# Order of gather and scatter in GpSimd's queue, in the last stage of a four-layer graph network

## The chip, the core and the metric

The kernel runs on one core of a Trainium2 chip. The metric is the device time of one execution in microseconds (us), from the first to the last instruction with what lies around them. The core's engines are named as in the profile: PE (TensorE, matmuls; PEld is its weight load), DVE (VectorE), ACT (ScalarE), POOL (GpSimd, here almost only the issuer of indirect DMAs) and SP (SyncE, the issuer of plain DMAs). Each engine works through its own list of instructions and waits on semaphores for the others.

## The reference

A graph of 100,000 nodes with 64 features each and 50,000 edges (src, dst), sorted by dst, goes through four residual layers. LN is a layer norm over the 64 features, and `sum` adds up the edges of one destination node:

```
h = relu(LN(x));  x = x + S(S(h))             S(h)[d] = sum(edge_weight * h[src])
h = relu(LN(x));  x = x + norm * sum(norm * (h @ W)[src]) + self loop + bias
h = relu(LN(x));  x = x + relu((h + sum(h[src])) @ W1.T + b1) @ W2.T + b2
h = relu(LN(x));  m = relu([h[src], h[dst], edge_attr] @ mW1 + mb1) @ mW2 + mb2
                  x = x + relu([h, sum(m)] @ uW1 + ub1) @ uW2 + ub2
```

All matrices are small (64 to 160 rows, 64 or 128 columns) and all data float32.

## The kernel before, in words

The edges lie in 128 partitions by 392 columns (391 and one more), in order of their destination. A *unit* is 14 columns (`G`), that is 128 x 14 edges; there are 28 units, and a *step* is two of them, b = 0 and b = 1, so 14 steps (`STEPS`), numbered 0 to 13. Every tile that is written as `name[b]` exists once for each b and serves all the steps: `ga[b]`, `acc[b]`, `isl[b]` and `osl[b]` among them.

The stages follow each other: preparation and ranks, two hops of layer 1 with scattered sums, a dense pass that computes all layers for all nodes as if they had no edges and writes `out`, two passes that sum the messages of layers 2 and 3 into `tables[0]` and `tables[1]`, and the **last stage**, which the change touches. It takes the edges from the last column to the first, computes for each edge layers 2 and 3 of its source and its destination, layer 4 with the message network (`m0`, `m1`: two halves of seven columns) and the update network (`u0`, `u1`), and scatters the new rows of those nodes that have edges to `out`.

The last stage is software-pipelined on PE, ACT and DVE. Each of the three runs `last_pass(None)` once and then `last_pass(i)` for i = 0 to 13; this text calls them *pass* i. In pass i an engine finishes step i (messages, running sums, update network) and in between prepares step j = i + 1. What matters here, in the order of the lists:

- DVE, pass i: line 2031 adds `us[b] = hin[b] + ga[b]` for step i + 1, where `ga` holds the gathered sums of `tables[1]`. When both additions are done it raises `ga_free` of step i + 1 (each b by itself). Later come the running sums of step i + 1 over `x3[b]` (line 1658, tile `zx`), which overwrite `x3` and so wait for `acc_ready` of step i; between that of b = 0 and that of b = 1 the update's first half is added to `acc` (line 1998, `u0`). The second half (`u1`) is added last in the pass, and then `o_ready` of step i is raised: `acc[b]` holds the finished rows.
- ACT, pass i: after its work for step i + 1 it copies `acc[b] = x3[b]` for b = 0 and b = 1 (line 1441) and raises `acc_ready`. Before each copy it waits until the scatter of step i - 1 has landed, since that reads `acc[b]`. Behind the two copies in its list stand the PSUM copies and rectifiers of the update network:

```
if not first:
    act.wait_ge(tt.written[b], 16 * G * i)
tt.acc_ready.raise_by(nc.scalar.copy(flat(acc[b]), flat(x3[b])), ("a", b))
...
copy(tt, i, "u0")
relu(tt, i, "u0", 2)
```

- PE, pass i: transposes and matmuls in the order m0, m1, the products of step i + 1, u0, u1.
- SP loads the tiles of step i + 2 in pass i and stores the running message sums.
- POOL: `t_gather(j)` waits for `ga_free` of step j - 1 for b = 0, copies 14 indices to `isl[0]` (line 768), issues 14 indirect DMAs of 128 rows into `ga[0]` (line 772), and does the same for b = 1. `t_scatter(i)` waits for `o_ready` of step i, copies indices to `osl[b]` and issues 14 indirect DMAs from `acc[b]` to `out` (line 908), for b = 0 and then b = 1. Before, the list was: gather 0, 1, 2, scatter 0, gather 3, then for i = 2 to 11 in a loop scatter i - 1 and gather i + 2, then scatters 11, 12, 13.

Of the kernel before, what the change touches and what calls it, by code (L numbers as in the profile page):

```python
# [126 lines left out]
def gnn(nc, x, src, dst, edge_attr, edge_weight, W1g, b1g, W2a, b2a, W2b, b2b, mW1, mb1, mW2, mb2, uW1, ub1,  # L127
        uW2, ub2, out):
    ctx = ExitStack()
    with ctx:  # L130
# [344 lines left out]
        def tcol(i, b):  # L475
            return (U - 1 - b) * G - 2 * G * i
# [230 lines left out]
        def _(pool):  # L707
# [58 lines left out]
            def slot_copy(o, i_):  # L766

                return nc.gpsimd.tensor_copy(o, i_).then_inc(s_slot, 1)  # L768

            def gather(o, table, idx, limit, s, columns=range(G)):  # L770
                for g in columns:
                    nc.gpsimd.indirect_dma_start(  # L772
                        o[:, g, :], None, table, bass.IndirectOffsetOnAxis(idx[:, g:g + 1], 0),
                        bounds_check=limit, oob_is_err=False).then_inc(s, 16)
# [116 lines left out]
            def t_gather(i, slots, first=False):  # L891
                for b in B2K:
                    if not first:
                        after.wait_ge(*tt.ga_free.at(i - 1, ("g", b)))
                    slot_copy(isl[b][:, :], ptr_i[:, bass.ds(tcol(i, b), G)])
                    after.wait_ge(s_slot, base + slots + b + 1)
                    gather(ga[b], tables[1], isl[b], rows_max, tt.got_a[b])

            def t_scatter(i, slots, first=False):
                for b in B2K:  # L900
                    after.wait_ge(*tt.o_ready.at(i, ("o", b)))
                    if not first:

                        after.wait_ge(tt.written[b], 16 * G * i)
                    slot_copy(osl[b][:, :], out_idx[:, bass.ds(tcol(i, b), G)])
                    after.wait_ge(s_slot, base + slots + b + 1)
                    for g in range(G):
                        nc.gpsimd.indirect_dma_start(  # L908
                            out, bass.IndirectOffsetOnAxis(osl[b][:, g:g + 1], 0), acc[b][:, g, :], None,
                            bounds_check=nodes_max, oob_is_err=False).then_inc(tt.written[b], 16)  # L910
# [3 lines left out]
            t_gather(0, 0, True)  # L914
            t_gather(1, 2)
            t_gather(2, 4)
            t_scatter(0, 6, True)
            t_gather(3, 8)
            with pool.Fori(2, STEPS - 2) as i:
                t_scatter(i - 1, 4 * i + 2)  # L920
                t_gather(i + 2, 4 * i + 4)
            for i in (STEPS - 3, STEPS - 2, STEPS - 1):
                t_scatter(i, 2 * STEPS + 2 * i)

# [1216 lines left out]
```

## Time and profile before

| what | value |
|---|---|
| time, median of 3 runs | 6286.37 us (6284.91 to 6287.19) |
| the profiled execution: its time | 6285.3 us |
| its span, first to last instruction | 6283.5 us |
| POOL busy, share of the span | 3393.1 us, 54% |
| PE busy | 3762.4 us, 60% |
| DVE busy | 3494.4 us, 56% |
| ACT busy | 1775.1 us, 28% |
| the last stage: from its first gather, 4870 us, to the end | about 1,413 us |
| the same stretch, busy: PE, DVE, POOL, ACT | 1008, 965, 876, 531 us |

Shares of busy time average over stages with different limits. The rows further down are of the last stage and show one pass in the middle of it, the first passes and the last. In a row of the timeline the first number is the start in us from the start of the span, the second the duration, then the engine, the line, the operation, the tiles (output before the arrow) and how many instructions are merged; in brackets stands how long the engine was idle before, and what ended that.

### The profile page before, as it was taken

Reading aid. Unit: us, or ns where it says so; the run is one execution under the profiler, and the core shown is the slowest. Engines: PE = TensorE matmul, PEld = TensorE weight load, DVE = VectorE, ACT = ScalarE, POOL = GpSimd, SP = SyncE. Lnnn points to the kernel's source line nnn. Section 1 sums busy time; section 2 is a strip of 40 time slices with the busy share of each in tenths; the row PEclk is TensorE's granted clock in tenths of the full one; section 3 lists DMA queues with packets and bytes.
Section 4 is the critical chain, followed back from the end, with each engine's and each line's share of the span. In section 5 each row is a group of like instructions: output and inputs, shape, how many; then the busy total and the mean of one; then the engine's idle time right before and its main releaser. Section 6 shows DMA issues by size and latency. Waiting matters only on the chain.

```text
span 6283.5 us, 70156 instructions
## 1 busy us (share of the span) xinstructions
PE 3762.4 (60%) x19038; PEld 3090.1 (49%) x19150; DVE 3494.4 (56%) x7361; ACT 1775.1 (28%) x3984; POOL 3393.1 (54%) x2949
## 2 busy tenths in 40 slices
PE   4756665654888888788888830001211577777775
PEld 2444444434888888666666630001111466666664
DVE  5434434433444444578888854443555677777773
ACT  2433443430000000344444420000100334434432
POOL 3777777764555555400000037767775566766763
PEclk9766666665555555699999975555555788888887
DMA  3232223232222222211111112222333322222220
GB/s 121 48 57 48 48 48 57 48 66 25 24 23 23 23 24 21 42 47 47 47 47 47 47 62 94 94 102 99 133 124 124 108 71 88 92 64 88 94 62 16
DMA packets 318644, 398.99 MB, mean 63 GB/s; under 512 B 206217, under 2 KB 223719, under 8 KB 317990
## 3 DMA queue, kind: packets, MB, share of 16 engines
q1 hardware_dynamic: 142518, 309.97, 14.0%
q0 software_dynamic: 176000, 87.72, 10.8%
q14 instruction: 93, 0.76, 0.0%
q8 instruction: 33, 0.54, 0.0%
HBM read 219.85 MB, written 212.39 MB: 69 GB/s over the span
## 4 chain that ended last, share of the span: by engine, by line
PE 24%; issue 21%; POOL 20%; DVE 16%; DMA 10%; ACT 4%; DVEq 1%; POOLq 0%; SPq 0%; ACTq 0%
POOL ga L772 14%; DMA hop<-acc,osl 8%; PE tp L1095 6%; PE tp L1082 5%; POOL hop L810 4%; PE tp L967 4%; PE mm L1015 3%; DVE xc L1620 2%; PE mm L948 2%; DVE cc L1658 2%; DVE wide L1799 1%; PE tp L941 1%; DVE st L1617 1%; DVE h L1640 1%; DVE wide L1794 1%
## 5 line engine op out<-in xcount | busy, mean ns | idle before, releaser
L772 POOL DMA_INDIRECT ga<-table,isl x784 | 836.3, 1067 | 271.5 <-issue 231.0
L846 POOL DMA_INDIRECT xu<-acc,osl x392 | 613.7, 1566 | 488.8 <-issue 452.7
L810 POOL DMA_INDIRECT hop<-acc,osl x392 | 632.8, 1614 | 194.4 <-issue 130.8
L1256 ACT ACTIVATE sq<-xc 128x896 f32<-128x896 f32 x280 | 266.2, 951 | 1289.6 <-DVE xc L1620 1283.6
L768 POOL COPY isl<-map_idx 128x14 int32 (+1 forms) x28 | 6.4, 228 | 1082.0 <-DMA ms<-h 1080.7
L1082 PE MATMUL tp<-us,wide 128*128 128x64 f32 x1568 | 416.9, 422 | 268.3 <-DVE wide L1799 268.3
L1029 PE MATMUL tp<-us,wide 128*128 128x64 f32 x1568 | 341.1, 422 | 369.2 <-DVE us L1640 369.2
L1029 PEld LDWEIGHTS tp<-us,wide 128*128 128x128 f32 x1568 | 336.6, 333 | 376.5 <-issue 376.5
L1082 PEld LDWEIGHTS tp<-us,wide 128*128 128x128 f32 x1568 | 380.0, 332 | 276.5 <-DVE wide L1799 166.5
L1617 DVE TENSOR_REDUCE st<-ga 128x14 f32<-128x896 f32 x56 | 60.8, 1085 | 781.9 <-DMA ga<-in_x,isl 610.1
L908 POOL DMA_INDIRECT out_x<-acc,osl x392 | 422.8, 1079 | 133.9 <-issue 113.0
L772 POOL DMA_INDIRECT ga<-in_x,isl x392 | 414.9, 1058 | 119.8 <-issue 81.4
L772 POOL DMA_INDIRECT ga<-xu,isl x392 | 401.6, 1025 | 138.9 <-issue 117.8
L1794 DVE TENSOR_SCALAR wide<-mm,key_slot 128x256 f32<-128x256 f32 x392 | 188.0, 480 | 510.8 <-PE mm L1019 475.1
L1044 PE MATMUL tp<-xw,cc 128*128 128x394 f32 x784 | 396.6, 599 | 93.7 <-ACT found L1350 93.4
L1095 PE MATMUL tp<-acc,wide 128*128 128x64 f32 x1560 | 423.4, 427 | 0.8
L1375 ACT ACTIVATE acc<-tp,h 128x64 f32<-128x64 f32 x392 | 101.5, 310 | 1072.7 <-PE tp L1095 958.9
L1267 ACT COPY vt<-tp 128x896 f32<-128x896 f32 x224 | 199.4, 906 | 684.2 <-PE tp L941 682.5
L1095 PEld LDWEIGHTS tp<-acc,wide 128*128 128x128 f32 x1560 | 372.4, 329 | 20.2 <-ACT acc L1375 5.5
L941 PE MATMUL tp<-ident,us 128*128 128x128 f32 x392 | 84.9, 404 | 486.7 <-DVE us L1929 486.5
L1000 PE MATMUL tp<-acc,mh 128*128 128x64 f32 x4 | 1.3, 435 | 577.4 <-DMA hsum<-table,head_i 577.4
L1626 DVE TENSOR_REDUCE st<-sq 128x14 f32<-128x896 f32 x280 | 294.5, 1085 | 76.2 <-ACT sq L1256 74.6
(327 smaller groups left out, 9332.6 us busy)
## 6 DMA issues: line engine op xcount, KB each, us to landing
wide<-xu SPq DMA_DIRECT2D x56, 448.0 KB, 3.3
table<-acc SPq DMA_DIRECT2D x56, 448.0 KB, 2.5
xin<-xs SPq DMA_DIRECT2D x56, 448.0 KB, 4.5
wide<-table SPq DMA_DIRECT2D x56, 448.0 KB
xu<-in_x SPq DMA_DIRECT2D x25, 1000.0 KB, 5.7
hop<-zeros SPq DMA_DIRECT2D x1, 12544.0 KB, 35.6
xu<-ga SPq DMA_DIRECT2D x28, 448.0 KB, 2.6
hin<-hop SPq DMA_DIRECT2D x28, 448.0 KB, 3.3
```

The costliest lines, as they stand in the source:

```text
L772: nc.gpsimd.indirect_dma_start(o[:, g, :], None, table, bass.IndirectOffsetOnAxis(idx[:, g:g + 1], 0), bounds_check=limit, oob_is_err=Fals ...
L810: nc.gpsimd.indirect_dma_start(hop, bass.IndirectOffsetOnAxis(osl[b][:, g:g + 1], 0), acc[b][:, g, :], None, bounds_check=hop_max, oob_is_ ...
L846: nc.gpsimd.indirect_dma_start(xu, bass.IndirectOffsetOnAxis(osl[b][:, g:g + 1], 0), acc[b][:, g, :], None, bounds_check=all_max, oob_is_e ...
L908: nc.gpsimd.indirect_dma_start(out, bass.IndirectOffsetOnAxis(osl[b][:, g:g + 1], 0), acc[b][:, g, :], None, bounds_check=nodes_max, oob_i ...
L967: t = nc.tensor.matmul(o[:, at - c + j * w:at - c + j * w + w], src_[:, j * P:j * P + P], weights, start=False, stop=j == (c + n) // w - 1)
L1029: t = nc.tensor.matmul(o[:, g * D:g * D + D], equal[b][:, c, (g % 2) * P:(g % 2) * P + P], us[b][:, c, :], start=n == 0, stop=n == 1)
L1044: f.key_row.raise_by(nc.tensor.matmul(tp[1][:, at:at + KEYS], reach[:, g * P:g * P + P], key_steps, start=True, stop=True), ("g", b, g))
L1082: t = nc.tensor.matmul(o, equal_run[:, 2 * q + n, mine:mine + P], us[b][:, 2 * q + n, :], start=n == 0, stop=alone and n == 1)
L1095: t = nc.tensor.matmul(o, equal_run[:, c, 2 * P + mine:3 * P + mine], passed[:, c, :], start=False, stop=n == 1)
L1256: f.squared.raise_by(nc.scalar.activation(full(lane_s[q]), full(lane_c[q]), ACT.Square), (n, q))
L1626: f.variance.raise_by(V.tensor_reduce(st[q][:, 1, :], full(lane_s[q]), X, ALU.add), (n, q))
L1794: V.tensor_scalar(equal_run[:, g, 0:2 * P], mm[half][:, here * P:here * P + 2 * P], key_slot[b][:, g:g + 1], None, ALU.is_equal)
```

## The change

In POOL's list the gather of the sums two steps ahead is put ahead of the scatter of the results one step behind, in the loop and in the two items ahead of it. The second argument is the number of index copies made so far, on which each waits, and follows the order. Nothing else changes, and the other engines' lists are the same.

```
@@ -914,11 +914,11 @@
             t_gather(0, 0, True)
             t_gather(1, 2)
             t_gather(2, 4)
-            t_scatter(0, 6, True)
-            t_gather(3, 8)
+            t_gather(3, 6)
+            t_scatter(0, 8, True)
             with pool.Fori(2, STEPS - 2) as i:
-                t_scatter(i - 1, 4 * i + 2)
-                t_gather(i + 2, 4 * i + 4)
+                t_gather(i + 2, 4 * i + 2)
+                t_scatter(i - 1, 4 * i + 4)
             for i in (STEPS - 3, STEPS - 2, STEPS - 1):
                 t_scatter(i, 2 * STEPS + 2 * i)
```

## Rows read from the trace of the kernel before

**Rows 1.** The page, GpSimd's busy tenths in 40 slices; the last stage is the last nine.
```profile
POOL 3777777764555555400000037767775566766763
```

**Rows 2.** Waits from 5000 us on: who waited for whom, total us, times, longest.
```profile
POOL osl L768 <- DVEq L75: 206.9, 14, 53.0
...
ACT acc L1441 <- DMA out_x<-acc,osl: 11.9, 1, 11.9
```

**Rows 3.** Line 2031 on VectorE over the whole run.
```profile
L2031 DVE TENSOR_TENSOR us<-hin,ga x28: 1082/1086/1093, 4909.4 to 6115.8; 128x896 f32<-128x896 f32 x28
its engine sat idle before it (us, times) until:
```

**Rows 4.** VectorE in order of time, one pass: start, us, engine, line, operation, idle before.
```profile
5459.80 2.09 DVE L2031 TENSOR_TENSOR us<-hin,ga 128x896 f32<-128x896 f32 x2
...
5498.28 1.14 DVE L1658 SCALAR_TENSOR_TENSOR zx<-zx,more,wide 128x64 f32<-128x64 f32 x3
...
5553.35 2.10 DVE L2031 TENSOR_TENSOR us<-hin,ga 128x896 f32<-128x896 f32 x2
```

**Rows 5.** GpSimd in order of time, the same pass.
```profile
5423.97 0.19 POOL L768 COPY osl<-out_idx 128x14 int32 x1 [10.47 <-DVEq L75]
...
5465.31 0.23 POOL L768 COPY isl<-ptr_i 128x14 int32 x1
5466.40 1.99 POOL L772 DMA_INDIRECT ga<-table,isl  x1 [0.86 <-POOL isl L768]
...
5517.48 0.19 POOL L768 COPY osl<-out_idx 128x14 int32 x1 [10.47 <-DVEq L75]
```

**Rows 6.** ScalarE in order of time, the same pass.
```profile
5485.21 1.77 ACT L1441 COPY acc<-zx 128x896 f32<-128x896 f32 x2
5489.67 1.90 ACT L1267 COPY vt<-tp 128x896 f32<-128x896 f32 x2 [2.69 <-PE tp L941]
```

**Rows 7.** Pass 13, the chain that ended last.
```profile
6207.43 2.15 DMA out_x<-acc,osl
```

**Rows 8.** GpSimd, its two DMA lines: ns, minimum, median and maximum of one.
```profile
L772 POOL DMA_INDIRECT ga<-table,isl x784: 991/997/1985, 4240.7 to 6066.2; - x196
...
L908 POOL DMA_INDIRECT out_x<-acc,osl x392: 982/983/1911, 5050.5 to 6264.5; - x196
```

**Rows 9.** Gather of step 2 in pass 0: VectorE's line 2031, then GpSimd.
```profile
4994.91 2.09 DVE L2031 TENSOR_TENSOR us<-hin,ga 128x896 f32<-128x896 f32 x2
...
4996.13 0.93 POOL L768 COPY isl<-ptr_i 128x14 int32<-128x14 int32 x1 [45.30 <-DVEq L75]
...
4999.95 1.00 POOL L772 DMA_INDIRECT ga<-table,isl  x1 [0.30 <-issue]
```

**Rows 10.** Pass 13, GpSimd and ScalarE in order of time.
```profile
6171.99 0.20 POOL L768 COPY osl<-out_idx 128x14 int32<-128x14 int32 x1 [52.97 <-DVEq L75]
6172.46 0.98 POOL L908 DMA_INDIRECT out_x<-acc,osl  x1 [0.28 <-POOL osl L768]
...
6196.74 0.94 ACT L1441 COPY acc<-zx 128x896 f32<-128x896 f32 x1
6209.60 0.94 ACT L1441 COPY acc<-zx 128x896 f32<-128x896 f32 x1 [11.92 <-DMA out_x<-acc,osl]
```

**Rows 11.** TensorE, then VectorE: first row of the pass above, the others of pass 13.
```profile
5490.63 3.27 PE L948 MATMUL mm<-vt,u 128*128 128x512 f32 x8
...
6211.39 5.74 PE L948 MATMUL mm<-vt,u 128*128 128x512 f32 x8 [5.12 <-ACT vt L1267]
...
6220.56 0.62 DVE L1998 TENSOR_TENSOR acc<-acc,tp 128x448 f32<-128x448 f32 x1 [1.07 <-PE tp L967]
```

**Rows 12.** Pass 13 by windows: busy us (instructions) by engine, PEclk, DMA share, GB/s.
```profile
6211.00:6216.00 5.00, 4.61 (x6) 2.19 (x7) 0.00 (x0) 2.15 (x3) 0.00 (x0) 0.50 0.00 0
...
6217.30:6230.00 12.70, 11.62 (x82) 9.46 (x80) 2.49 (x4) 4.70 (x5) 0.63 (x2) 1.00 0.00 1
```

**Rows 13.** The chain of waits from 5400 to 5600, shares by line.
```profile
by line: issue 26.5%; PE tp L967 14.8%; PE mm L948 8.8%; DVE cc L1658 8.3%; DVE zx L1658 5.9%; PE mm L952 4.7%; DVE xc L1620 4.5%; PE tp L941 4.2%; ACT zx L1272 4.1%; DVEq L1658 2.9%; PE tp L965 2.1%; DVE us L2051 2.0%; DVE h L2046 1.3%; DV
```

## The prediction

> **What bounds the kernel now.** I read the page first, for where the changed stage lies and how full POOL is in it [rows 1]: five to seven tenths in most slices, so POOL is not the bound there. The waits of the stage say the same from both sides. POOL stands 207 us in all in front of its scatters, for `o_ready`, while ACT waits only once for a scatter, 11.9 us, and that once is the very last pass [rows 2]. Line 2031, which consumes the gathers, is never idle before it starts [rows 3]: the gathers are early enough in all 14 steps. What sets the stage is the cycle DVE, ACT, PE. One pass from line 2031 to line 2031 takes 5553.35 - 5459.80 = 93.55 us [rows 4].
>
> Then I laid one pass of POOL beside it. The scatter of the step behind starts at 5423.97, right at the end of the pass before, and the gather follows at 5465.31, so a scatter takes 41.3 us of POOL. The next scatter starts at 5517.48 after 10.47 us of idleness, so the gather ended at 5507.0 and took 41.7 us [rows 5]. ACT copies `acc` at 5485.21 [rows 6], and the scatter that reads `acc` has been issued by 5465.3. Its last DMA lands 2.15 us after its start [rows 7], that is 1.2 us after the 0.98 us [rows 8] for which POOL is busy with it. So there are now 18.7 us of slack between the scatter's landing and ACT's first copy. The change has to be measured against this slack.
>
> **The change part by part.** It removes and adds no instruction: 28 gathers, 28 scatters and four index copies for each step stay, and SP's queue is untouched. It moves the scatter of step i - 1 behind the gather of step i + 2 and behind that gather's wait.
>
> *When the gather can start.* It waits for `ga_free` of step i + 1, raised in the same pass i, after line 2031. The gather of step 2, which had no scatter ahead of it, shows this: POOL stood 45 us and started at 4996.13, 1.22 us after line 2031 started at 4994.91 [rows 9]. In the pass shown [rows 4] that is 5459.80 + 1.22 = 5461.0, against 5465.3 now. The gather wins 4.3 us that nobody needs [rows 3].
>
> *When the scatter lands.* `o_ready` has been up since 5424, but the scatter now stands behind the gather: 5461.0 + 41.7 = 5502.7. Its length I take from pass 13, where DVE was mostly idle, as it will be here: from the index copy at 6171.99 to the landing, which released ACT at 6209.60, 37.6 us [rows 10]. In the loop the first DMA comes 1.09 us after its index copy [rows 5], outside it 0.47 [rows 10], so two times 0.62 are added: 38.8 us. The scatter has landed at 5502.7 + 38.8 = 5541.5.
>
> *Who waits.* ACT's second `acc` copy began at 5485.21 + 1.77 - 0.94 = 5486.0 (0.94 is one copy alone [rows 6, 10]). It now begins at 5541.5: 55.5 us later. ACT's list stands behind it (the copies and rectifiers of `u0` and `u1`), PE stands for ACT, and DVE stands in front of the running sums over `x3`, for `acc_ready`. All four engines are then behind this one landing, because everything of step i + 1 that doesn't need it has been done by 5486. POOL itself has nothing to do afterwards, since its next gather needs the next line 2031. So the delay is not absorbed by the following pass; it comes again in each.
>
> *What is given back.* In pass 13 of the kernel before this very wait occurs once. From the start of the released copy, 6209.60, to the end of the `u0` additions, 6220.56 + 0.62, where the running sums of b = 1 would start, it took 11.6 us [rows 10, 11]. Undisturbed it is 5498.28 - 5486.04 = 12.2 us [rows 4, 6]. The 2.69 us for which ACT now waits for the transposes of `u0` [rows 6] are gone, since PE has made them meanwhile; against that the first product after the standstill takes 5.74 instead of 3.27 us [rows 11]. Net 0.7 us with rounding. From there to the next line 2031 everything shifts rigidly. One pass grows by 55.5 - 0.7 = 54.8 us, to 148.
>
> *How many passes.* In the new order the scatters 0 to 10 stand behind the gathers 3 to 13, and their landings are awaited in passes 1 to 11: eleven. Scatters 11 and 12 have no gather ahead of them, as before, and start at `o_ready`; the end of the stage is the same. The first of the eleven is outside the loop, 2.5 us cheaper (four times 0.62). Sum: 11 x 54.8 - 2.5 = 600 us on the profiled execution's own 6285.3, that is 6886 us. The runs' median is 1.1 us above that execution, which changes nothing here.
>
> *Bounds of the terms.* The gather can at best be free of disturbance: 14 x (1.00 + 0.30) + 1.09 = 19.3 for each b [rows 5, 8, 9], 38.6 for both, 3.1 us less, or 34 us over eleven passes. The scatter can at worst be as slow as it is today under a busy DVE: 41.3 + 1.2 = 42.5, 3.7 us more, or 41 us. The restart after the standstill can cost PE a second product of the same kind, 2.5 us more, or 27 us; in pass 13 TensorE was granted 0.50 of its clock, that is the 1.2 GHz level, for the first 5 us and 1.00, the 2.4 GHz level, from 6217.3 on [rows 12], so I leave this out of the sum. That gives 6852 to 6954 for this case.
>
> The trace shows single scatters between 0.98 and 1.91 us [rows 8], the long ones under a busy DVE and none in pass 13's first scatter. The Trainium skill ("SBUF — State Buffer", "SBUF: two separate sides") says that a VectorE instruction with two SBUF inputs and a GpSimd operation that reads SBUF exclude each other for the whole instruction. By that rule the scatter, moved to where DVE stands, runs undisturbed, and the sum is the 6886 above; without it the scatter stays at today's length and the sum would be 6927. I follow pass 13, which is the case itself.
>
> **The rivals.**
>
> *Only half of the wait counts.* The copy of `acc[0]` waits only for the scatter's first half. If the pass could go on from there, with b = 1 catching up later, the landing would be 5502.7 + 19.4 = 5522.1 against 5485.2, 36.9 - 0.7 = 36.2 us in each pass, and the time 6285 + 398 = 6684. Against it: ACT's copy of `acc[1]` stands ahead of all `u0` work in its list, and in pass 13 nothing of `u0` moved between 6196.74 and 6209.60 [rows 10, 11].
>
> *PE stays slow after each standstill.* If the clock did not come back soon, all matmuls on the cycle would run at the lower level. PE's lines hold 14.8 + 8.8 + 4.7 + 4.2 + 2.1 = 34.6% of the chain [rows 13], 32 us of a pass; at the ratio 5.74 / 3.27 that is 24.6 us more for each of eleven passes, and the time 6886 + 271 = 7157. For it: PE would be idle for some 50 us in each pass. Against it: in pass 13 the level was back within 8 us [rows 12].
>
> *Not slower.* This needs one mechanism: the gather's release comes a pass earlier than I read it. Both orders would fit into POOL's idle time if the gather could start by 5485.2 - 41.7 - 19.4 = 5424.1 for b = 0, or 5486.0 - 41.7 - 38.8 = 5405.5 for both. So it decides at a release about 55 us before the one that I read, and then the time is 6285, since no gather is late now and nothing can be gained. Against it: step 2's gather started 1.2 us after line 2031 and not earlier, though POOL had stood for 45 us [rows 9]. The data demand it as well, for line 2031 reads the buffer that the gather fills.
>
> **How the numbers follow.** The case of the sum gets 0.86, the half wait 0.05, the slow PE 0.05, and no effect 0.03; 0.01 remains for something faster. The prediction is that of the likeliest, 6886. Its own bounds, 6852 to 6954, hold nearly all of its 0.86, and I widen them by some 10 us on both sides: 6840 to 6965. A measurement of this kernel tells about 0.2%, 13 us, from no change. Slower by more: 0.96. Within: 0.03. Faster: 0.01.
>
> **What the profile of the changed kernel would show.** Right, if: ACT's copy in line 1441 waits for the landing of a scatter eleven times more, the second copy about 55 us after today's phase, and the wait table puts some 610 us on "acc, line 1441, waits for the DMA to out", split over two copies; line 2031 starts 148 us apart in the middle of the stage; POOL waits before `isl` and no longer before `osl`, about 69 us each time; DVE stands in front of line 1658's `zx`; and line 2031 still never waits for a gather. Each term by itself: gather 41.7, scatter with landing 38.8, from released copy to the end of the `u0` additions 11.6. Wrong, if line 1441 doesn't wait, if `u0` work starts before the second copy, if PEclk in the stage is far below 0.85, or if line 2031 starts to wait for `ga`.

## The result, and the profile after

The changed kernel takes 6887.78 us (median of 4 runs, 6884.82 to 6889.23) against 6285.64 us of the kernel before (4 runs): ratio 1.0958, 95% interval [1.0939, 1.0977], 602 us more. The forecast was 6886 us. The profiled execution spans 6884.8 us. One execution of a version further down took 9522 us at a granted clock of 0.44 instead of 0.69 and is left out of its median and ratio.

The waits of the stage, in the same form as [rows 2]:

```profile
POOL isl L768 <- DVEq L75: 743.7, 11, 69.9
ACT acc L1441 <- DMA out_x<-acc,osl: 630.0, 23, 39.2
...
DVE zx L1658 <- ACT acc L1441: 363.0, 11, 34.1
```

ScalarE's wait for the scatter's landing has grown from 11.9 us, once, to 630.0 us in 23 waits: two in each of eleven passes and the one of pass 13 that was there before. The waits of POOL have changed place: it now stands 743.7 us, eleven times, before the index copy of the gather, and before that of a scatter only in the last three. VectorE stands behind ScalarE. Line 2031 waits for a gather once, 1.2 us, at 4909.65, where it takes up step 0; no gather of the changed part is late:

```profile
L2031 DVE TENSOR_TENSOR us<-hin,ga x28: 1082/1088/1093, 4907.3 to 6723.6; 128x896 f32<-128x896 f32 x28
...
  DMA ga<-table,isl: 1.2, 1
```

Its start, which stood 93.5 us apart [rows 4], now stands 147 to 150 us apart in the eleven passes. One of them, first POOL (as [rows 5]):

```profile
5678.69 0.61 POOL L768 COPY isl<-ptr_i 128x14 int32 x1 [69.31 <-DVEq L75]
...
5700.36 0.20 POOL L768 COPY isl<-ptr_i 128x14 int32 x1
...
5720.44 0.21 POOL L768 COPY osl<-out_idx 128x14 int32 x1
...
5739.26 0.24 POOL L768 COPY osl<-out_idx 128x14 int32 x1
...
5826.40 0.61 POOL L768 COPY isl<-ptr_i 128x14 int32 x1 [68.35 <-DVEq L75]
```

POOL is idle for 69 us (the bracket of the first row); then come the gather from 5678.69 to 5720.44, 41.75 us, and the scatter at once behind it. ScalarE in the same pass (as [rows 6, 10]):

```profile
5740.50 0.94 ACT L1441 COPY acc<-zx 128x896 f32<-128x896 f32 x1 [37.85 <-DMA out_x<-acc,osl]
5759.24 0.94 ACT L1441 COPY acc<-zx 128x896 f32<-128x896 f32 x1 [17.81 <-DMA out_x<-acc,osl]
5760.09 1.71 ACT L1267 COPY vt<-tp 128x896 f32<-128x896 f32 x2
```

The first copy waited 37.85 us and the second 17.81 us more, until 5759.24, which is 38.8 us after the scatter's start. The copies of `u0` follow without a wait. VectorE (as [rows 4]):

```profile
5677.15 2.09 DVE L2031 TENSOR_TENSOR us<-hin,ga 128x896 f32<-128x896 f32 x2
...
5741.69 0.28 DVE L1658 SCALAR_TENSOR_TENSOR zx<-zx,more,wide 128x64 f32<-128x64 f32 x1 [32.81 <-ACT acc L1441]
...
5769.28 0.62 DVE L1998 TENSOR_TENSOR acc<-acc,tp 128x448 f32<-128x448 f32 x1 [1.16 <-PE tp L967]
...
5824.86 2.09 DVE L2031 TENSOR_TENSOR us<-hin,ga 128x896 f32<-128x896 f32 x2
```

The running sums over `x3` of b = 0 start when the first copy is done, after 32.81 us of waiting; those of b = 1 stand behind the additions at 5769.28, and so behind the second copy. The next line 2031 comes 147.7 us after the last. TensorE's first product after the standstill (as [rows 11]), in the pass before and in this one; behind the two rows stand the windows of both (as [rows 12]; the column before the last two is the granted clock):

```profile
5612.36 5.67 PE L948 MATMUL mm<-vt,u 128*128 128x512 f32 x8 [54.32 <-ACT vt L1267]
```

```profile
5761.04 4.72 PE L948 MATMUL mm<-vt,u 128*128 128x512 f32 x8 [53.07 <-ACT vt L1267]
```

```profile
5611.00:5616.00 5.00, 3.64 (x5) 1.85 (x6) 0.00 (x0) 2.36 (x4) 0.00 (x0) 0.50 0.00 0
...
5760.00:5765.00 5.00, 3.96 (x7) 1.94 (x8) 0.00 (x0) 2.50 (x4) 0.00 (x0) 0.60 0.00 0
5765.00:5770.00 5.00, 4.93 (x40) 4.33 (x38) 1.34 (x3) 1.35 (x3) 0.00 (x0) 1.00 0.00 0
```

It takes 5.67 and 4.72 us instead of 3.27. The granted clock is 0.50 (the 1.2 GHz level) just after the standstill, and in the second pass 1.00 (the 2.4 GHz level) again within 6 us of the first product. Over a whole pass, first of the kernel before and then of the changed one, the same columns are:

```profile
5459.80:5553.35 93.55, 70.71 (x423) 57.80 (x426) 68.85 (x119) 37.86 (x52) 62.95 (x60) 0.88 0.26 82
```

```profile
5677.15:5824.86 147.71, 73.88 (x426) 58.81 (x426) 69.03 (x119) 37.97 (x52) 60.08 (x60) 0.74 0.17 52
```

The mean granted clock of the pass has fallen from 0.88 to 0.74, but the low part of it lies in the standstill (0.50 from 5742 to 5759, with no matmul); TensorE's busy time has grown by 3.2 us. Finally the two groups of GpSimd's DMAs in the middle of the stage; the second figure behind the bar is the mean time of one:

```profile
L772 POOL DMA_INDIRECT ga<-table,isl x267 | 298.7, 1119 | 96.6 <-issue 80.0 <-POOL isl L768 16.5
L908 POOL DMA_INDIRECT out_x<-acc,osl x269 | 265.0, 985 | 95.3 <-issue 80.0 <-POOL osl L768 15.3
```

### The profile page after: what moved, and what is told of

It reads as the page before. It is cut to its first block, busy times and chain, and to the rows that moved or that the text cites. A ratio compares the mean times of both kernels' runs of the same rounds, so it can differ in the third digit from the quotient of the medians.

```text
span 6884.8 us, 70268 instructions
## 1 busy us (share of the span) xinstructions
PE 3807.1 (55%) x19150; PEld 3092.7 (45%) x19150; DVE 3497.2 (51%) x7361; ACT 1777.7 (26%) x3984; POOL 3360.3 (49%) x2949
## 4 chain that ended last, share of the span: by engine, by line
POOL 28%; PE 23%; issue 20%; DVE 13%; DMA 9%; ACT 4%; DVEq 1%; POOLq 0%; SPq 0%; ACTq 0%
POOL ga L772 18%; DMA hop<-acc,osl 7%; PE tp L1095 5%; POOL out_x L908 5%; PE tp L1082 5%; POOL hop L810 4%; PE tp L967 4%; PE mm L1015 2%; PE mm L948 2%; DVE cc L1658 2%; DVE xc L1620 1%; DVE wide L1799 1%; DVE st L1617 1%; PE tp L941 1%; DVE wide L1794 1%
## 5 line engine op out<-in xcount | busy, mean ns | idle before, releaser
L908 POOL DMA_INDIRECT out_x<-acc,osl x392 | 389.4, 993 | 133.8 <-issue 114.8
L1044 PE MATMUL tp<-xw,cc 128*128 128x394 f32 x784 | 402.4, 609 | 93.8 <-ACT found L1350 93.1
L948 PE MATMUL mm<-vt,u 128*128 128x512 f32 x224 | 118.0, 682 | 595.0 <-ACT vt L1267 595.0
L768 POOL COPY isl<-ptr_i 128x14 int32 (+1 forms) x56 | 30.9, 552 | 813.5 <-DVEq L75 810.9
```

The lines of the kernel that those rows point to most:

```text
L908: nc.gpsimd.indirect_dma_start(out, bass.IndirectOffsetOnAxis(osl[b][:, g:g + 1], 0), acc[b][:, g, :], None, bounds_check=nodes_max, oob_i ...
L948: t = nc.tensor.matmul(o[:, c:c + n], weights, flat(src_)[:, c:c + n], start=True, stop=extra is None)
L1044: f.key_row.raise_by(nc.tensor.matmul(tp[1][:, at:at + KEYS], reach[:, g * P:g * P + P], key_steps, start=True, stop=True), ("g", b, g))
```

## The experiments

All experiments ran beside runs of the kernel before on the same chip. On the chip of four of the kernels (the cut gathers and scatters, and the repetition of the kernel before) the kernel before took 6293 us, near the result above; on the three others it took 6569, 6572 and 6724 us, with nothing changed in it. None of these four was used on two occasions, so whether this belongs to the chip or to the occasion is not shown; the text names each by its time. What is different there is the subject of the last part below. Times are therefore given as a ratio, or as a difference of the medians, to the kernel before on the same chip, and the traces are compared by the phase within a pass: how long after line 2031 ScalarE's second `acc` copy starts (26.2 us undisturbed: 5486.04 - 5459.80), and what remains from there to the next line 2031 (67.3 us undisturbed).

**Only the pair outside the loop.** The loop keeps the old order, only the two calls ahead of it are exchanged.

```
-            t_scatter(0, 6, True)
-            t_gather(3, 8)
+            t_gather(3, 6)
+            t_scatter(0, 8, True)
             with pool.Fori(2, STEPS - 2) as i:
                 t_scatter(i - 1, 4 * i + 2)
                 t_gather(i + 2, 4 * i + 4)
```

> Only the pair outside the loop is in the new order (gather 3, then scatter 0); the loop has the old one. Theory of the late landing: pass 1 alone waits, 54.8 - 2.5 = 52 us, and all later passes are as before, so 6286 + 52 = 6338. Rival (the cost is a restart or a slower clock that spreads over the stage): clearly more than 52. Rival (the loop's own order of waits costs it, not the first standstill): 6286.

Measured on the 6569 us chip: ratio 1.0036 [1.0012, 1.0061], that is 24 us with an interval of 8 to 40. The forecast 52 is missed. The trace has the wait itself as forecast, in pass 1 (36.2 and 17.3 us) and in no other:

```profile
ACT acc L1441 <- DMA out_x<-acc,osl: 53.5, 2, 36.2
```

The wait has the place and the length that were forecast; its price in time is not confirmed. In this trace pass 1 takes 166.2 us from line 2031 to line 2031, and the ten behind it 107 to 118. That looks like a price of some 50 us, but the runs say 24, and those of the kernel before spread over 66 us on this chip, where it has no trace.

**Where each half of the scatter stands.** The loop and the pair ahead of it take the units b = 0 and b = 1 one by one, in three orders (g is the gather of step i + 2, s the scatter of step i - 1):

```
             with pool.Fori(2, STEPS - 2) as i:
-                t_scatter(i - 1, 4 * i + 2)
-                t_gather(i + 2, 4 * i + 4)
+                t_gather(i + 2, 4 * i + 2, bs=(0,))
+                t_scatter(i - 1, 4 * i + 3, bs=(0,))
+                t_gather(i + 2, 4 * i + 4, bs=(1,))
+                t_scatter(i - 1, 4 * i + 5, bs=(1,))
```

This is the order g0 s0 g1 s1; the others are g0 s0 s1 g1 and s0 g0 s1 g1.

> Order in the loop and in the pair ahead of it: gather b = 0, scatter b = 0, gather b = 1, scatter b = 1. The last landing lies where it lies in the changed kernel, 80.5 us after the gather's start; that of b = 0 comes 20 us earlier. Theory (the landing of b = 1, the last, sets the pass): the same as the changed kernel, 6887. Rival (the pass goes on from the landing of b = 0, which is 1.5 + 21.7 + 18.8 + 1.2 = 43.2 us after line 2031 instead of the 25.4 that ACT would need): 11 x 17.1 = 188 more than before, 6474.

> Order: gather b = 0, scatter b = 0, scatter b = 1, gather b = 1. Theory: the last landing is 20 us earlier than in the changed kernel, 62.0 us after line 2031 against the 26.2 needed, so 35.1 us a pass, 386 in all, 6670. Rival of the first half: 6474, as in the run before. Rival (POOL's standstill before the gather is what costs, wherever the scatter stands): 6887.

> Order: scatter b = 0, gather b = 0, scatter b = 1, gather b = 1. The scatter of b = 0 is where it was before the change. Theory: the landing of b = 1 is 1.5 + 21.7 + 20.0 = 43.2 us after line 2031 against 26.2 needed, 16.3 us a pass, 6465, up to 6480 if the scatter is slowed by the busy DVE as before the change. Rival of the first half: 6286, nothing changes. Rival of POOL's standstill: 6887.

ScalarE's two copies in one pass of each, in this order (in s0 g0 s1 g1 the first copy doesn't wait):

```profile
5629.43 0.94 ACT L1445 COPY acc<-zx 128x896 f32<-128x896 f32 x1 [21.60 <-DMA out_x<-acc,osl]
5665.82 0.94 ACT L1445 COPY acc<-zx 128x896 f32<-128x896 f32 x1 [35.45 <-DMA out_x<-acc,osl]
```

```profile
5705.10 0.94 ACT L1445 COPY acc<-zx 128x896 f32<-128x896 f32 x1 [21.65 <-DMA out_x<-acc,osl]
5721.14 0.94 ACT L1445 COPY acc<-zx 128x896 f32<-128x896 f32 x1 [15.10 <-DMA out_x<-acc,osl]
```

```profile
5664.98 0.93 ACT L1445 COPY acc<-zx 128x896 f32<-128x896 f32 x1
5686.64 0.94 ACT L1445 COPY acc<-zx 128x896 f32<-128x896 f32 x1 [20.73 <-DMA out_x<-acc,osl]
```

Line 2031 of the same passes starts at 5582.33, 5657.94 and 5639.58. All on the 6569 us chip:

| order | second copy after line 2031, expected / measured | waits of ScalarE | ratio to the kernel before | difference |
|---|---|---|---|---|
| g0 s0 g1 s1 | 82 / 83.5 us | 616.7 us in 22 | 1.0627 [1.0562, 1.0691] | 416 us |
| g0 s0 s1 g1 | 62.0 / 63.2 us | 407.7 us in 22 | 1.0344 [1.0276, 1.0411] | 230 us |
| s0 g0 s1 g1 | 43.2 / 47.1 us | 231.5 us in 11 | 1.0191 [1.0125, 1.0258] | 130 us |

The time follows the landing of the last half. In the third order the second half lands 3.9 us later than expected; its difference is measured with two runs alone. Of the rivals, the first half's landing would make the first two orders equal, and the third free; both are wrong, and in g0 s0 g1 s1 the first half lands 36 us before the second, and the pass still waits for the second. POOL's standstill before the gather goes with the time (69.5, 51.1 and 16.8 to 26.3 us in these passes), and the rival by which it costs the same wherever the scatter stands (6887 for all three) is wrong: the three orders differ by up to 286 us. It is what remains of the pass. The absolute differences are smaller than the 602, 386 and 179 expected for a chip like the first. The passes of the loop, read at line 2031, are not shorter than expected: 148 to 151 us with g0 s0 g1 s1 and 131 to 135 with g0 s0 s1 g1, against 149 of the changed kernel on the first chip and 128.6 by the sum. It is the kernel before that is slower there.

**Cutting the gather or the scatter.** Each of the two in the loop is cut to one DMA for each b, which raises the semaphore by as much as all fourteen; the other 13 columns are not gathered, or not written.

```
-                    for g in range(G):
+                    for g in range(dmas):
...
-                            bounds_check=nodes_max, oob_is_err=False).then_inc(tt.written[b], 16)
+                            bounds_check=nodes_max, oob_is_err=False).then_inc(tt.written[b], 16 * G // dmas)
...
-                t_scatter(i - 1, 4 * i + 2)
+                t_scatter(i - 1, 4 * i + 2, dmas=1)
```

> The order of before; in the loop each scatter issues one DMA for each b instead of 14 (steps 1 to 10 leave out the other 13 columns), which raises the semaphore by 14 times as much. Theory (the scatter has slack in the old order): on a chip like the first nothing changes, 6286. Where passes of the kernel before take 106 to 110 us: if the scatter's issue is what makes the other engines idle there, its ten passes fall back towards 94 and the time is 100 to 150 us below the kernel before; if not, the same as before.

> The order of before; in the loop each gather issues one DMA for each b instead of 14 (steps 4 to 13 leave out the other 13 columns). Theory (the gathers are early enough): on a chip like the first 6286. On one like those of the last calls: the same as the kernel before if only the scatter's place matters for the idle time, 100 us less or more below it if any indirect DMA of GpSimd does it.

Measured on the 6293 us chip: 0.9999 [0.9988, 1.001] and 0.9998 [0.9987, 1.001]. In the old order neither the 260 scatter DMAs nor the 260 gather DMAs that are left out are worth anything, and pass 13's wait stays in both:

```profile
ACT acc L1441 <- DMA out_x<-acc,osl: 12.3, 1, 12.3
```

```profile
ACT acc L1441 <- DMA out_x<-acc,osl: 11.5, 1, 11.5
```

So both have slack in the old order, and the change had nothing to win. The second part of these expectations, on the slower chips, was not tested, since this chip was not one of them. The same cut of the gather in the changed order:

> The changed order with the gathers of the loop cut to one DMA for each b, as in the run before, so that the scatter stands behind the gather's wait but hardly behind its work. Theory: the scatter starts about 1.5 + 3.5 us after line 2031 and lands 38.8 us later, 43.8 against 26.2 needed: ScalarE waits some 17 us in each of the ten passes instead of 55, a pass takes about 111 us, and pass 1 costs its 52 us: about 6508 on a chip like the first. Rival (only the place behind the gather's wait counts, not its length): ScalarE waits 55 us as in the changed kernel, 6887.

Measured: 6577.68 us, ratio 1.0451 [1.0421, 1.0481], 285 us above the kernel before. The direction is right and the rival of the place alone is wrong (6887), but the size was about 60 us short (6508 - 6286 = 222 expected, 285 measured). One pass, POOL, then ScalarE, then the mean of the scatter's DMAs:

```profile
5708.68 0.61 POOL L768 COPY isl<-ptr_i 128x14 int32 x1 [71.58 <-DVEq L75]
...
5713.44 0.20 POOL L768 COPY osl<-out_idx 128x14 int32 x1
...
5734.70 0.23 POOL L768 COPY osl<-out_idx 128x14 int32 x1
```

```profile
5738.94 0.94 ACT L1441 COPY acc<-zx 128x896 f32<-128x896 f32 x1 [6.29 <-DMA out_x<-acc,osl]
5758.11 0.94 ACT L1441 COPY acc<-zx 128x896 f32<-128x896 f32 x1 [18.24 <-DMA out_x<-acc,osl]
```

```profile
L908 POOL DMA_INDIRECT out_x<-acc,osl x273 | 297.3, 1089 | 92.8 <-issue 77.5 <-POOL osl L768 15.4
```

The two index copies and two DMAs of the gather take 4.8 us where 3.5 were expected, so the scatter starts 6.3 us after line 2031 (5713.44 - 5707.14) and not 5.0. And it takes 44.7 us from 5713.44 to 5758.11 instead of the 38.8 that I carried over from pass 13: here it runs while VectorE is busy, and one DMA takes 1089 ns on the average, against 985 ns in the changed kernel. The two errors, 1.3 and 5.9 us, make up the whole difference. The second copy starts 51.0 us after line 2031 instead of 43.8: 51.0 - 26.2 - 0.7 = 24.1 us in each of ten passes and 52 in pass 1 are 293 us, against the 285 measured.

**Taking the wait away, not the order.** POOL first copies `acc` to a buffer of its own, scatters from there as late as in the changed kernel, and ScalarE waits for that copy.

```
+            def t_stage(i, first=False):
+                for b in B2K:
+                    after.wait_ge(*tt.o_ready.at(i, ("o", b)))
+                    if not first:
+                        after.wait_ge(tt.written[b], 16 * G * i)
+                    nc.gpsimd.tensor_copy(stage[b][:, :, :], acc[b][:, :, :]).then_inc(staged, 1)
...
             with pool.Fori(2, STEPS - 2) as i:
+                t_stage(i - 1)
                 t_gather(i + 2, 4 * i + 2)
                 t_scatter(i - 1, 4 * i + 4)
...
-                            act.wait_ge(tt.written[b], 16 * G * i)
+                            act.wait_ge(staged, 2 * i + b - 1)
```

> The changed kernel's order of gather and scatter, but POOL first copies acc of the finished step into a buffer of its own (two copies of 128x896, before the gather's wait), scatters from there, and ACT waits for that copy and no longer for the scatter's landing. The scatters are issued as late as in the changed kernel. Theory of the late landing: ACT doesn't wait, the stage is as before the change, and pass 13 loses its 11.9 us as well; the copies, which I estimate at 1 to 4 us each since no row shows one of this size, lie in POOL's idle time save for those of the last step: 6275 to 6290. Rival (the late scatter or POOL's standstill itself costs the time): near 6887.

Measured on the 6572 us chip: ratio 1.0122 [1.0091, 1.0152]; the medians differ by 90 us. ScalarE doesn't wait for a landing at all any more, and the copies are cheap (minimum, median and maximum in ns):

```profile
L906 POOL COPY stage<-acc x28: 924/930/1572, 5113.3 to 6615.4; 128x896 f32<-128x896 f32 x28
```

With the scatter as late as in the changed kernel, the passes take 110 to 134 us instead of 147 to 150. So it is the buffer that the late scatter holds that costs most of the time, and not the scatter's lateness. But the forecast of "as before" is missed by some 80 to 90 us, and for these a cost of the late scatter itself, in idle time like the following, is not excluded. VectorE, while POOL issues the scatter (5681 to 5720), and then while POOL is idle (5723 to 5758):

```profile
5694.15 2.08 DVE L1635 TENSOR_REDUCE st<-sq 128x14 f32<-128x896 f32 x2 [2.52 <-issue]
5700.69 0.44 DVE L1638 RECIPROCAL st<-st 128x14 f32<-128x14 f32 x2 [4.46 <-issue]
...
5713.00 0.62 DVE L2007 TENSOR_TENSOR acc<-acc,tp 128x448 f32<-128x448 f32 x1 [7.18 <-remote]
...
5745.47 5.00 DVE L1667 SCALAR_TENSOR_TENSOR cc<-cc,cont,us 128x64 f32<-128x64 f32 x12 [0.16 <-DVE cc L1667]
```

The first three stand behind 2.52, 4.46 and 7.18 us of idleness that the profile can't lay to any engine of this core; the group of twelve at the end runs without a gap. In other passes of this trace the idle time lies elsewhere too, up to 39.9 us of it at once on ScalarE. The last part comes back to it.

**The scatter in two halves.** The old order, but the first seven columns of each scatter are issued as soon as the first half of the update is in `acc`:

```
...
+                for half in range(2):
+                    for b in B2K:
+                        if half:
+                            after.wait_ge(*tt.o_ready.at(i, ("o", b)))
+                        else:
+                            after.wait_ge(*tt.taken.at(i, ("u0", b)))
+                        for g in range(half * HB, half * HB + HB):
...
```

> The kernel before, with its order, but each scatter issues the first seven columns of both b as soon as the update's first half (u0) has been added to acc, and the other seven after the second half. Theory: in the middle of the stage there is slack on both sides of the scatter, so nothing changes there; in pass 12 the scatter starts about 18 us earlier and the only wait of ACT (11.9 us, pass 13) goes; after pass 13 some 8 us of the last scatter move ahead of its end. 6286 - 12 - 8 = 6266, between 6262 and 6272. Rival (GpSimd's work under a busy VectorE slows the cycle): 6286 or more.

Measured on the 6572 us chip: ratio 0.992 [0.989, 0.9949], 49 us less, more than the 20 expected. It is the only version that is faster than the kernel before; on a chip like the first it was not run. Of the two terms the trace shows the last one. The additions of `u0` and of the last `u1` in pass 13, on VectorE:

```profile
6457.38 0.62 DVE L2002 TENSOR_TENSOR acc<-acc,tp 128x448 f32<-128x448 f32 x1 [7.25 <-PE tp L971]
...
6472.94 0.62 DVE L2002 TENSOR_TENSOR acc<-acc,tp 128x448 f32<-128x448 f32 x1 [5.06 <-remote]
```

and the chain that ended last, where the 28 DMAs of the last scatter start:

```profile
6458.78 0.98 POOL out_x L912
```

It starts 14.8 us before the last addition is done (6472.94 + 0.62). The wait of pass 13 doesn't occur, but neither did it in the other traces of such chips, so it can't be the gain there. The remaining 34 us are not explained; the runs of the kernel before spread over 72 us on that chip.

**The slower chips.** 

> The changed kernel once more, beside the kernel before on the chip of this call. On the chips of the last two calls the kernel before took 6570 us instead of 6286, its engines idling more inside a pass with nothing that the profile shows to wait for. Theory: the standstill for the scatter's landing is set by POOL's 80.5 us and not by those idle times, and hides part of them; so on such a chip the change costs less than 602, about as much as the order g0 s0 g1 s1 did (416), and on a chip like the first 602 again. Rival (the two orders differ by their first half's landing): the changed kernel costs clearly more than 416 where that order costs 416.

> The order gather b = 0, scatter b = 0, scatter b = 1, gather b = 1 once more, beside the changed kernel on one chip. Theory: on a chip like the first 6670, 386 above the kernel before; on one like those of the last two calls about 230 above it, as there. Rival of POOL's standstill: as slow as the changed kernel.

> The kernel before once more, for its trace on a chip like those of the experiments. Theory: there the passes take 106 to 110 us instead of 93.5, and the additional idle time of VectorE, ScalarE and TensorE lies where GpSimd issues the scatter, not where it is idle. Rival: it is spread evenly over the pass.

The first two ran on the 6724 us chip: ratio 1.0499 [1.0457, 1.0541], 327 us, for the changed kernel, and 1.0319 [1.028, 1.0358], 207 us, for g0 s0 s1 g1. So the change costs less than 602 there, as expected, but also less than the 416 of g0 s0 g1 s1 on the other chip; and the two orders, which on one chip differ by 120 us, show POOL's standstill wrong as the cause once more. The third ran on the 6293 us chip (6294.02 us), with passes of 93.5 to 93.8 us, and so didn't show what it was meant for. But the question can be read from the windows of the others. The stretch from the second `acc` copy to the next line 2031, and the one from there to the next second copy. First the kernel before (first chip), then the loop of "only the pair", which is that of the kernel before (6569 us chip), then the changed kernel (6724 us chip), the first stretch only, in pass 3 and in pass 11. The columns are the length, the busy time of PE, its weight load, DVE, ACT and POOL with their instructions, the granted clock, and the DMAs' share and rate:

```profile
5486.00:5553.30 67.30, 52.07 (x327) 43.65 (x326) 45.10 (x92) 24.12 (x32) 42.44 (x42) 0.88 0.21 65
5553.30:5579.50 26.20, 19.44 (x98) 14.42 (x101) 23.70 (x27) 13.60 (x21) 20.16 (x20) 0.85 0.40 125
```

```profile
5543.20:5626.40 83.20, 56.39 (x312) 45.59 (x310) 45.09 (x93) 24.09 (x32) 44.62 (x43) 0.77 0.18 53
5626.40:5652.60 26.20, 20.12 (x118) 15.62 (x117) 23.74 (x27) 13.58 (x21) 18.74 (x18) 0.93 0.40 125
```

```profile
5584.20:5650.50 66.30, 50.35 (x295) 41.11 (x296) 35.81 (x72) 23.96 (x31) 0.00 (x0) 0.83 0.03 7
...
6779.80:6859.16 79.36, 56.07 (x295) 46.07 (x296) 35.84 (x73) 24.04 (x31) 30.71 (x30) 0.75 0.06 15
```

The second stretch takes 26.2 us on both chips. The first takes 67.3 us on the first chip and 83.2 on the slower one, with the same busy time of DVE and ACT. In the changed kernel it takes 66.3 us although the chip is the slowest of all: POOL issues nothing in it. The loop's passes were 147 to 151 us there, as on the first chip. The last row shows the exception in the same execution: in pass 11 no gather stands ahead of the next scatter, so that POOL's scatter lies in this stretch again, and it takes 79.4 us, where the ten passes before have 66 to 67 and the same pass on the first chip has 65.8 (6722.60 - 6656.77). The granted clock is lower in the long stretches (0.77 and 0.75 against 0.88 and 0.83) and TensorE is busy 4 to 6 us longer, so a part of the 13 to 16 us is TensorE's; whether that is cause or follows from the idling is not shown. By this the kernel before has about 16 us more in each pass on such chips, and the new order has them in one pass only: 55.9 - 16 = 40 us a pass, times eleven 440 us, an estimate from the loop of one trace, since the kernel before has no trace on such a chip. Measured were 416 for g0 s0 g1 s1 and 327 for the changed kernel. The rival that it is spread evenly over the pass is wrong. That POOL's scatter is the cause is not shown: the test, leaving it out on such a chip, was not made. Why engines idle there and not beside the gather in the 26.2 us stays open: the profile has no releaser for this time.

## Why the prediction was right

The places, the mechanism and the size of the steps, in the prediction's order:

- *When the gather can start.* Predicted 1.22 us after line 2031; measured 5678.69 - 5677.15 = 1.54.
- *When the scatter lands.* Gather 41.7 predicted, 41.75 measured; scatter with landing 38.8 predicted, 5759.24 - 5720.44 = 38.8 measured. The second copy starts 82.1 us after line 2031 instead of 26.2: 55.9 us against 55.5. In six of the ten passes of the loop it starts 83.3 or 83.4 us after it, and in each of these one DMA is issued 1.5 us after the end of the one before it instead of 0.3, for a reason that the profile doesn't show. One of them:

```profile
5851.63 1.84 POOL L772 DMA_INDIRECT ga<-table,isl  x1 [1.51 <-issue]
```

That the scatter would be fast under a standing VectorE is borne out by the mean of one DMA, 985 ns, where it was 1089 ns in the experiment that moved it under a busy one. The traces also tell which VectorE instructions lengthen a DMA. GpSimd and VectorE beside each other:

```profile
5691.34 1.70 POOL L772 DMA_INDIRECT ga<-table,isl  x1 [0.30 <-issue]
5693.35 0.99 POOL L772 DMA_INDIRECT ga<-table,isl  x1 [0.30 <-issue]
```

```profile
5691.09 2.08 DVE L2046 TENSOR_TENSOR h<-h,wide 128x896 f32<-128x896 f32 x2
5693.10 2.08 DVE L2051 TENSOR_TENSOR us<-xin,tp 128x896 f32<-128x896 f32 x2
```

`h` and `wide` both lie in SBUF, `tp` in PSUM. From 5000 us on, 134 of GpSimd's indirect DMAs in this trace overlap a 128x896 instruction with two inputs in SBUF, and 73 of these take more than 1.15 us, up to 1.90; of the 589 others, beside a wide reduction, a wide addition with one input in PSUM, narrow instructions or nothing, none takes more than 1.08. The Trainium skill ("SBUF — State Buffer", "SBUF: two separate sides") says that GpSimd's reads and a VectorE instruction with two SBUF inputs exclude each other; by that rule the DMAs that lengthen are these, and the trace agrees (1.70 against 0.99 us).
- *Who waits.* ScalarE, then TensorE and VectorE, as named. The rival of the half wait is shown wrong by the first copy, which ran 18.7 us before the second and released the running sums of b = 0 but not `u0`, and by the three orders above.
- *What is given back.* Predicted 0.7 us. From the second copy to the end of the `u0` additions it took 11.6 us in the pass with the 5.67 us product, as in pass 13 [rows 10, 11], and 10.66 in the one shown above. The remainder of the pass is 66.6 and 65.6 us against 67.3, so 0.7 or 1.7. The rival of the slow TensorE is shown wrong by the clock's windows and by its busy time, 3.2 us more in a pass where that rival had some 24 (its 24.6 should read 24.4). The recorded sign against the forecast, a granted clock far below 0.85 in the stage, was badly put: the mean did fall to 0.74, by the standstill itself, and from 5765 us to the end of the pass it is 0.86.
- *How many passes.* Eleven. Their intervals add up to 1640.0 us against 1029.4, 610.6 more, where the sum had 600. The six late DMAs, 1.2 us each, and the 0.4 us in each of the ten passes of the loop account for that (11 us). Outside them 9 us went the other way: 2.7 us in the first passes of the stage and its start, and 6.5 us from the last line 2031 to the end of the span, 5.5 of it behind the last scatter's start (6229.09 to 6283.5 before, 6835.88 to 6884.8 after). So the agreement within 2 us with the measured median is in part luck: 10.6 us too little in the passes, 9 too much elsewhere.

*Not slower* is shown wrong too: the gather did start 1.5 us after line 2031, and cutting gather or scatter in the old order shows that there was nothing to win. What the sum did not know is how much it depends on the chip: on the 6724 us chip the same change costs 327 us. The traces point to idle time that the kernel before has there and the new order's standstill doesn't repeat; its cause is open.

## What to carry to other kernels

Before an engine's list is reordered, look at what each item holds while it waits: a scatter that is ready early but stands behind an item that becomes ready late holds its source buffer all that time, and the price is the landing's new phase minus the phase at which the buffer's next writer comes, once in each iteration. An idle time of the issuing engine is no sign that moving its work is free. Where a kernel has the wait once already, in a last or first iteration, that iteration gives the terms of the sum that nothing else shows, here the scatter's length beside a standing VectorE and the restart.

## What the runs showed of the hardware

- The same scatter of 28 DMAs with its landing took 42.5 us in the old order (41.3 + 1.2), 44.7 us when it was issued 6 us after line 2031, with VectorE busy, and 38.8 us with VectorE mostly standing.
- An indirect DMA of GpSimd was lengthened, from 0.98 or 1.00 us to as much as 1.90, only beside a 128x896 float32 VectorE instruction with both inputs in SBUF (73 of 134); beside one with an input in PSUM it was not (39, the longest 1.07), nor beside a wide reduction (60, the longest 1.03).
- A copy of 128x896 float32 on GpSimd took 0.93 us (median of 28), the same as ScalarE's 0.94.
- One indirect DMA can raise its semaphore by 224 in place of fourteen that raise it by 16 each; the waits behind it were satisfied as before.
- The kernel before took 6286, 6293, 6569, 6572 and 6724 us on five occasions. Where it is slow, a pass of its loop has its additional time in one stretch (83.2 instead of 67.3 us), the larger part of it idle time without a releaser. In one execution of the changed kernel that stretch took 66 to 67 us in ten passes in which GpSimd issued nothing, and 79.4 us in the one in which it issued a scatter.
